# Graph attention on one core: the two large products by one level of Strassen's algorithm

## The reference

```python
h = relu(layernorm(x))                      # 64 x 128 x 512
output = h @ weight ; q = h @ wq ; k = h @ wk
alpha = q @ k.T                             # per graph, 128 x 128
alpha = softmax(max(alpha, 0) * (adj != 0), axis=1)
x = x + alpha @ output
```

## Time and profile before

| | |
|---|---|
| time, median of 3 runs | 454.89 us (454.82 to 455.75) |
| the profiled execution's own time | 454.48 us |
| its span, first to last instruction | 452.6 us |
| busy: TensorE, VectorE, ScalarE, GpSimd | 97%, 51%, 42%, 34% |
| chain that ended last | 95% on TensorE |
| granted TensorE clock, mean | 0.996 of full |

### The profile page before, as it was taken

One profiled execution on the slowest core, in us unless ns is written; L12 is line 12 of the kernel. 1 busy time (PEld: TensorE's weight loads), 2 busy tenths in 40 slices (PEclk: granted clock), 3 DMA queues, 4 the chain that ended last, 5 costly groups with the idle time before them and its releaser, 6 DMA issues.

```text
span 452.6 us, 7240 instructions
## 1 busy us (share of the span) xinstructions
PE 438.3 (97%) x2563; PEld 223.3 (49%) x2563; DVE 230.2 (51%) x448; ACT 190.3 (42%) x397; POOL 152.8 (34%) x203
## 2 busy tenths in 40 slices
PE   6959899999999999999999999999999999999996
PEld 4424545454544545454554545454454545445452
DVE  4793537263644726363562736355372636444254
ACT  4526282625245362515436262533626252453231
POOL 0412453605244250624334060534416062442002
PEclk9989999999999999999999999999999999999999
DMA  8960607373754718174552807364370827253022
GB/s 298 373 129 0 128 2 187 128 192 122 174 141 93 224 24 243 46 185 127 123 190 51 252 10 204 109 163 150 72 241 12 234 68 194 27 95 104 1 93 93
DMA packets 103266, 60.00 MB, mean 133 GB/s; under 512 B 77137, under 2 KB 85329, under 8 KB 103249
## 3 DMA queue, kind: packets, MB, share of 16 engines
q1 hardware_dynamic: 102672, 58.73, 48.4%
q10 hardware_dynamic: 576, 1.05, 0.6%
HBM read 24.12 MB, written 16.78 MB: 90 GB/s over the span
## 4 chain that ended last, share of the span: by engine, by line
PE 95%; DVE 3%; DMA 1%; ACT 0%; issue 0%; DVEq 0%
PE bank L646 12%; PE bank L648 12%; PE bank L647 12%; PE bank L637 12%; PE bank L638 12%; PE bank L639 12%; PE s_bank L659 3%; PE s_bank L660 3%; PE s_bank L661 3%; PE bank L669 3%; PE bank L670 3%; PE bank L671 3%; PE bank L711 2%; PE wT_bank L692 1%; DMA wk_sb<-in_L_gnn_wk 1%; DVE w_lo L597 1%
## 5 line engine op out<-in xcount | busy, mean ns | idle before, releaser
L646 PE MATMUL bank<-w_hi,hT_hi 128*128 128x512 f16 x256 | 97.5, 381 | 4.6 <-DVE m_lo L601 4.6
L461 DVE SCALAR_TENSOR_TENSOR v_lo<-bank,v_hi 128x512 f16<-128x512 f32 x64 | 44.2, 691 | 112.9 <-ACT v_hi L360 111.4
L647 PE MATMUL bank<-w_lo,hT_hi 128*128 128x512 f16 x256 | 97.5, 381 | 0.0
L648 PE MATMUL bank<-w_hi,hT_lo 128*128 128x512 f16 x256 | 97.5, 381 | 0.0
L637 PE MATMUL bank<-hT_hi,m_hi 128*128 128x512 f16 x256 | 97.0, 379 | 0.0
L638 PE MATMUL bank<-hT_lo,m_hi 128*128 128x512 f16 x256 | 97.0, 379 | 0.0
L639 PE MATMUL bank<-hT_hi,m_lo 128*128 128x512 f16 x256 | 97.0, 379 | 0.0
L300 POOL TENSOR_TENSOR hn_lo<-h,hn_hi 128x512 f16<-128x512 f32 x64 | 73.2, 1156 | 51.9 <-ACT hn_hi L356 51.8
L466 DVE SCALAR_TENSOR_TENSOR tT_lo<-bank,tT_hi 128x512 f16<-128x512 f32 x64 | 44.2, 691 | 87.6 <-ACT tT_hi L364 87.6
L306 POOL TENSOR_TENSOR probs<-exps,row_inv 128x512 f32<-128x512 f32 x16 | 16.6, 1039 | 202.9 <-DVE row_inv L498 202.9
L373 ACT ACTIVATE exps<-alpha,shift_max,s_unscale 128x128 f32<-128x128 f32 x64 | 30.8, 482 | 96.8 <-DVE shift_max L487 96.6
(11 more groups left out here) (70 smaller groups left out, 467.2 us busy)
## 6 DMA issues: line engine op xcount, KB each, us to landing
x_sb<-in_x SPq DMA_DIRECT2D x16, 1024.0 KB, 5.8
out_h<-x_sb SPq DMA_DIRECT2D x64, 256.0 KB, 2.2
adj_sb<-in_adj SPq DMA_DIRECT2D x16, 256.0 KB, 6.1
w_sb<-in_L_gnn_weight SPq DMA_DIRECT2D x1, 1024.0 KB, 11.3
wk_sb<-in_L_gnn_wk ACTq DMA_DIRECT2D x2, 256.0 KB, 3.9
wk_sb<-in_L_gnn_wk SPq DMA_DIRECT2D x2, 256.0 KB, 3.7
wq_sb<-in_L_gnn_wq SPq DMA_DIRECT2D x2, 256.0 KB, 6.5
wq_sb<-in_L_gnn_wq ACTq DMA_DIRECT2D x2, 256.0 KB, 6.7
```

Of the source, the lines that this page charges most:

```text
L461: nc.vector.scalar_tensor_tensor(v_lo[:, b], bank[b][:], T_SCALE, v_hi[:, b], ALU.mult, ALU.subtract).then_inc(emptied, 1)
L646: nc.tensor.matmul(bank[b][:], hT_hi[:, s, b, k], w_hi[:, k], start=k == 0, stop=False)
L647: nc.tensor.matmul(bank[b][:], hT_hi[:, s, b, k], w_lo[:, k], start=False, stop=False)
L648: last = nc.tensor.matmul(bank[b][:], hT_lo[:, s, b, k], w_hi[:, k], start=False, stop=k == K - 1)
```

## The change

T and V of groups 1 to 15 are each made by one level of Strassen's algorithm (Winograd's form). Left operand, right operand and result are cut into quadrants: the left into two pairs of graphs by two halves of the features, the right into 256 x 256. Seven products of quadrants and of sums of quadrants, P1 to P7, replace the eight of the plain form. Each is 2 x 2 x 3 = 12 matmuls of 256 columns. Group 0 keeps the plain form.

- The sums of W and of M (T1 to T4) are made once, at the start: those of W by GpSimd, those of M by VectorE, and split into high and low parts.
- The sums of h (S1 to S4) are made in every group by VectorE (`sum_s1` to `sum_s4`), four operations on 128 x 512 fp32 with both inputs in SBUF. ScalarE takes their high parts (`hi_of_sum`), GpSimd their low parts (`lo_of_sum`), and two more DMA transposes turn them.
- P1 is used twice: ScalarE copies its bank into another (`copy_p1_t`, `copy_p1_v`) on which P6 is then added. P5 is copied to SBUF (`copy_p5_t`, `copy_p5_v`). VectorE adds it to P1+P6 (`sum_x_t`, `sum_x_v`) and to P1+P6+P7 (`sum_c22_t`, `sum_c22_v`); the latter goes to SBUF, and its high and low parts are taken from there.
- The order is new: a period g holds T(g), V(g), output(g-1) and last scores(g). Output(g-1) stands behind 8 of the 14 products, and output(15) behind everything.

TensorE's period, from the diff:

```diff
+            def period(i, j):
+                pe.wait_ge(hT_landed[s], 2 * 16 * turn(i, j))
+                product_t(s, N_P1, bank[TA][:], True)
+                pe.wait_ge(sT_landed[s], 2 * 16 * turn(i, j))
+                product_t(s, N_P5, bank[TE][:], True)
+                pe.wait_ge(v_split, 4 * g)
+                product_v(s, N_P1, bank[VA][:], True)
+                product_v(s, N_P5, bank[VE][:], True)
+                pe.wait_ge(t_copied, 2 * g - 1)
+                product_t(s, N_P2, bank[TA][:], False)
+                product_t(s, N_P6, bank[TB][:], False)
+                pe.wait_ge(v_copied, 2 * g - 1)
+                product_v(s, N_P2, bank[VA][:], False)
+                product_v(s, N_P6, bank[VB][:], False)
+                outs(g - 1)
+                pe.wait_ge(t_summed, 2 * g - 1)
+                product_t(s, N_P7, bank[TB][:], False)
+                product_t(s, N_P3, bank[TE][:], False)
+                pe.wait_ge(v_summed, 2 * g - 1)
+                product_v(s, N_P7, bank[VB][:], False)
+                pe.wait_ge(t_summed, 2 * g)
+                product_t(s, N_P4, bank[TB][:], False)
+                product_v(s, N_P3, bank[VE][:], False)
+                pe.wait_ge(v_summed, 2 * g)
+                product_v(s, N_P4, bank[VB][:], False)
+                pe.wait_ge(t_split, 4 * g + 4)
+                pe.wait_ge(out_read, GB * g - 2)
+                scores(g, s)
```

Sums and copies, one of each kind:

```diff
+            def sum_s1(g):
+                vec.wait_ge(h_made, GB * g + GB)
+                if not isinstance(g, int) or g > 1:
+                    vec.wait_ge(s_split, 4 * g - 4)
+                nc.vector.tensor_tensor(s32[:, S1], quadrant(1, 0), quadrant(1, 1), ALU.add).then_inc(s_made, 1)
...
+            def sum_c22_t(g):
+                vec.wait_ge(t_filled, made(g, N_P7))
+                nc.vector.tensor_tensor(c22_t, bank[TB][:], p5_t, ALU.add).then_inc(t_summed, 1)
...
+            def copy_p1_t(g):
+                act.wait_ge(t_filled, made(g, N_P1))
+                act.wait_ge(t_split, 4 * g)
+                nc.scalar.activation(bank[TB][:], bank[TA][:], ACT.Copy).then_inc(t_copied, 1)
```

GpSimd's period, and what its list begins with:

```diff
+            def period(g, j, nxt2=True):
+                normalise(g - 1)
+                if nxt2:
+                    layernorm_scales(g + 2)
+                    lows_of_h(g + 2, j % 2)
+                    lows_of_sums(g + 2, j % 2)
+            pool.wait_ge(w_loaded, 16)
+            nc.gpsimd.tensor_tensor(wt32[:, T1], w_sb[:, 0:HK, HD:], w_sb[:, 0:HK, :HD], ALU.subtract).then_inc(wt_summed, 1)
...
             pool.wait_ge(consts_made, 5)
             layernorm_scales(0)
```

More of the change, by code:

```diff
@@ new lines, in _ @@
+            for k in range(K):
+                act.wait_ge(m_split, k + 1)
+                nc.scalar.activation(m32[:, k], M_BANK[k], ACT.Copy, scale=m_scale[:]).then_inc(m_copied, 1)
+            hi_of_sum(1, 1, 0, S1)
+            hi_of_sum(1, 1, 1, S3)
+            hi_of_sum(1, 1, 2, S2)
+            hi_of_sum(1, 1, 3, S4)
+            act.wait_ge(wt_summed, 4)
+            for f in range(4):
+                nc.scalar.activation(wt_hi[:, f], wt32[:, f], ACT.Copy, scale=w_scale[:]).then_inc(wt_hi_made, 1)
@@ L442, in _ @@
             for g in REST:
-                group(g // UNROLL, g % UNROLL, nxt=g + 1 < G, nxt2=g + 2 < G)
+                period(g // UNROLL, g % UNROLL, nxt2=g + 2 < G)
+            exponentials(LAST)
         @block.vector
@@ new lines, in _ @@
+            sum_s1(2)
+            sum_s3(2)
+            sum_s2(2)
+            sum_s4(2)
+            period(0, 1)
+            with vec.Fori(0, TURNS) as i:
+                for j in range(LOOPED, LOOPED + UNROLL):
+                    period(i + j // UNROLL, j % UNROLL)
+            for g in REST:
+                period(g // UNROLL, g % UNROLL, nxt=g + 1 < G, nxt2=g + 2 < G)
+            softmax_shift(LAST, LAST % 2, LAST // 2 + 1)
+            softmax_sum(LAST)
+            for b in range(GB):
+                residual(LAST, LAST % UNROLL, b)
@@ new lines, in right, with product_t @@
+            def right(part, sums, b):
+                if isinstance(b, tuple):
+                    return part[:, HK * b[0]:HK * (b[0] + 1), HD * b[1]:HD * (b[1] + 1)]
+                return sums[:, b]
+            def product_t(s, n, dst, first):
+                a, b = OPERANDS[n]
+                ah, al = left(hT_hi, s, a), left(hT_lo, s, a)
+                bh, bl = right(m_hi, mt_hi, b), right(m_lo, mt_lo, b)
+                for c in range(HK):
+                    o = dst[:, c * HD:(c + 1) * HD].rearrange("p (b n) -> p b n", b=HG)
+                    cols = slice(c * N, (c + 1) * N)
+                    for k in range(HK):
+                        nc.tensor.matmul(o, bh[:, k, cols], ah[:, :, k], start=first and c == 0 and k == 0, stop=False,
+                                         skip_group_check=True)
+                        nc.tensor.matmul(o, bh[:, k, cols], al[:, :, k], start=False, stop=False, skip_group_check=True)
+                        last = nc.tensor.matmul(o, bl[:, k, cols], ah[:, :, k], start=False, stop=k == HK - 1,
+                                                skip_group_check=True)
+                last.then_inc(t_filled, 1)
@@ new lines, in product_v @@
+            def product_v(s, n, dst, first):
+                a, b = OPERANDS[n]
+                ah, al = left(hT_hi, s, a), left(hT_lo, s, a)
+                bh, bl = right(w_hi, wt_hi, b), right(w_lo, wt_lo, b)
+                for r in range(HG):
+                    o = dst[:, r * HD:(r + 1) * HD]
+                    for k in range(HK):
+                        nc.tensor.matmul(o, ah[:, r, k], bh[:, k], start=first and r == 0 and k == 0, stop=False,
+                                         skip_group_check=True)
+                        nc.tensor.matmul(o, ah[:, r, k], bl[:, k], start=False, stop=False, skip_group_check=True)
+                        last = nc.tensor.matmul(o, al[:, r, k], bh[:, k], start=False, stop=k == HK - 1,
+                                                skip_group_check=True)
+                last.then_inc(v_filled, 1)
@@ L664, in product_out @@
             def product_out(g, b):
[L666 to L684 removed]
+                dst = OUT_BANK[b]
@@ new lines, in product_out, with outs @@
+                nc.tensor.matmul(dst, p_hi[:, b], v_hi[:, b], start=True, stop=False)
+                nc.tensor.matmul(dst, p_hi[:, b], v_lo[:, b], start=False, stop=False)
+                nc.tensor.matmul(dst, p_lo[:, b], v_hi[:, b], start=False, stop=True).then_inc(out_filled, 1)
+            def outs(g, last=False):
+                pe.wait_ge(p_split, g + 1)
+                product_out(g, 0)
+                pe.wait_ge(scores_read, g + 1)
+                product_out(g, 1)
+                pe.wait_ge(t_split, 4 * g + (4 if last else 5))
+                product_out(g, 2)
+                pe.wait_ge(out_read, GB * g + 1)
+                product_out(g, 3)
```

649 lines of the change are left out of this document (404 added, 245 removed).

## The result

The changed kernel takes 529.0 us (median of 4 runs, 526.43 to 529.72) against 455.32 for the kernel before on the same chip (454.82 to 456.03): ratio 1.161, 95% interval 1.156 to 1.165. The profiled execution took 526.43 us with a span of 524.6, 72.0 longer than before.

The account below looks back on a forecast made before the run. TensorE bounds the kernel before; the change makes it wait on VectorE's list, lengthened by port waits. 73.8 + 34.1 + 12 x 28.4 + 2 x 23.6 + 15.1 = 511.0 us of span, forecast 513, own range 493 to 530, whole range 463 to 545.

Parts of the forecast that it names:

- TensorE's part: TensorE's matmuls of 256 columns: 0.109 us each, a half-size product 1.31, a period 23.6 us against 25.99 before.
- The port: VectorE operations with two SBUF inputs wait for the GpSimd operation in progress; the sums of h wait 3.1 us a period.
- the signs at the prediction's end: Sums of h well over 0.7 us, ending with GpSimd's hn_lo; VectorE's share of a period under 75%; scores(0) end near 74.
- The period, step by step: Chain through softmax, layernorm, h and VectorE's list to the scores: 28.4 us a period, TensorE stalled 4.8 of it.
- Rival 1: VectorE never waits at the port: periods of 25.3 us, time 464 us, still slower than before; chance 0.13.
- Start: Work before the first period: scores(0) start at 69.9 us and end at 73.8, where they ended at 56.0 before.
- Period 1: First period: 34.1 us, 5.7 more than the others, as GpSimd's low parts of group 2's sums precede layernorm(3).
- Periods 14 and 15: Last two periods, which have no sums of h: 23.6 us each.
- End: After the last scores: uncovered softmax 7.8, output 2.6, lower clock 1.25, hand-off 0.2 and 3.3 to the store: 15.1 us.
- The sum of periods 2 to 13: The twelve middle periods, counted at 28.4 us each.
- rival 2: TensorE's clock falls in every period after the stall ahead of P4 of V: 0.6 to 1.3 us each, 521 to 530; chance 0.14.
- Rival 3: VectorE's stretch from fourth residual to last tT_lo hides, under 6.9 us: periods of 23.6, time 442 us; chance 0.06.

Follow-up runs that it names:

- e1: Changed kernel with each sum of h from group 3 on reading one operand from PSUM, leaving out one summand: 487.3 us.
- e4: Changed kernel with the four sums of h made by GpSimd instead of VectorE, and ScalarE's high parts of sums moved later: 487.6 us.
- e3: Changed kernel with TensorE's loop of three turns over periods 2 to 13 written out, nothing else changed: 524.8 us.
- e7: Changed kernel with both the periods' order and the start reordered, TensorE's loop kept: 443.0 us, against 432.7 with that loop written out.
- e5: Changed kernel with sums of h last, c22 of T and V and ScalarE's first high part of V earlier, TensorE's loop written out: 450.2 us.

## Why the prediction came out right

- **TensorE's part**: right. Twelve matmuls of 256 columns start 0.109 us apart, a period without waits is 23.61 (predicted 23.6).
- **The port**: right in mechanism and size. Predicted extra waits of s1, s3, s2, s4: 0.4, 1.0, 0.8, 0.9 on top of 0.61; measured lengths 0.95, 1.64, 1.54, 1.52, which is 0.3, 1.0, 0.9, 0.9 over the 0.68 of one with a PSUM input. The turn that it read from operations on 128x1 (1.04 us after the start of one of 1.16 us on GpSimd) holds at full size: 1.04 + 0.68 is 0.56 after GpSimd's end, and the sums end 0.55 after it, not with it, as the signs at the prediction's end had it. e1, by one operand moved, and e4, where other operations with two inputs in SBUF were hit, show the cause. What the prediction lacks is GpSimd's side, a stretch of its operations of up to 0.45 us. The Trainium skill, in "SBUF — State Buffer", section "Who interferes with whom", has the rule that an instruction of VectorE with two SBUF inputs contends with one of GpSimd that reads SBUF. The runs agree at full size. The bounds for large operations (0 to 1.16 each) enclosed it.
- **The period, step by step**: right. s1 starts 14.06 us after the end of the scores before (269.93 less 255.87), as predicted, and the period is 28.38 against 28.4; stalls of 0.67, 2.81 and 0.58 against 1.0, 3.1 and 0.7. One sign missed by a little: VectorE's share of a period is 76% (21.56 of 28.38), not under 75%.
- **Rival 1** (no port, periods of 25.3, 464 us) is what e1 made in the periods, though not in the start: 25.70. It is slower than before, as the rival said. The rival's remark that start and end cost 26 us takes the start with the port; with its own 66.3 they come to 19. Its sum, 461.9, does not use the 26.
- **Start**: right. Scores(0) run from 70.0 to 74.2, predicted 69.9 to 73.8. **Period 1**, from the end of scores to the end of scores: 33.4 against 34.1. **Periods 14 and 15**: 23.61 each. **End**: 16.2 against 15.1; the lower clock lasts until 520.3, through three of the last output's four parts (residuals 1.28 us apart, then 0.65 at the full clock), and I had given it 1.25 us only.
- **The sum of periods 2 to 13**: predicted 340.8, measured 353.5. Two terms were missing, and they are 12.7 of the 16 us by which 529.0 lies above the 513 forecast (the end is 1.1 more of them, and the median lies 2.6 above the profiled execution). One is the jump of TensorE's loop, 7.3 us in periods 6 and 10. No row of before points to it: the middle periods there are 25.9 to 26.1, also those of the jump. e3 and e7 show it. The other is rival 2, in part: the clock falls not in every period but in every other, by 0.9 to 1.1 us, where the rival had 0.6 to 1.3; 5.8 in all. It falls at the place that the rival names: from 0.1 us ahead of the end of the stall of 2.8 us to 1.1 behind it, so that the last product of V and the scores run at the lower level. Less 0.4 (12 x 28.38 is 0.2 under the 340.8, and period 13 is 0.2 short) the two make up the 12.7; the span is 13.6 above the sum. The time alone would not tell the two stories apart: 529.0 lies just inside the forecast's own range (493 to 530) and inside rival 2's (521 to 530). The periods do: half of the middle ones have a full clock and 28.38 us, the forecast's 28.4. That the jump, which nobody had priced, didn't carry the time out of that range is luck.
- **Rival 3** (VectorE's stretch short enough to hide) was taken by its break-even point: below 24.5 us a period the change pays. The changed kernel is far from it, but e5 is below it with the same operations: the sums, for which TensorE does not wait at that place, are out of the stretch (and three of the four miss GpSimd where they now are). The prediction took the order of VectorE's list as given.

What stays open: why the jump costs nothing in the kernel before. It has fewer and longer matmuls (2563 on TensorE in all, against 3643), which could give the fetching of instructions more time; no run tested this.
